# Value bias of an attention kernel: added by VectorE, or by a one-row matmul on TensorE with copies on ScalarE

## The reference, cut to what matters

```python
x = x + jnp.tanh(g_xattn[l]) * xattn_l(_layernorm(x), ctx, ...)
x = x + jnp.tanh(g_ffn[l]) * ffn_l(_layernorm(x), ...)
```

```python
v = (V @ Wv.T + bv).reshape(B, S, H, Dh).transpose(0, 2, 1, 3)
out = softmax(q @ k.T * scale + mask) @ v
```

## Time and profile before

| what | us |
|---|---|
| median of three runs | 1249.05 |
| lowest and highest of the three | 1245.17, 1252.75 |
| the profiled execution | 1246.67 |
| its span, first to last instruction | 1244.9 |

### The profile page before, as it was taken

One profiled execution on the slowest core, in us unless ns is written; L12 is line 12 of the kernel. 1 busy time (PEld: TensorE's weight loads), 2 busy tenths in 40 slices (PEclk: granted clock), 3 DMA queues, 4 the chain that ended last, 5 costly groups with the idle time before them and its releaser, 6 DMA issues. The chain is left out here.

```text
span 1244.9 us, 28580 instructions
## 1 busy us (share of the span) xinstructions
PE 975.1 (78%) x9932; PEld 495.1 (40%) x9932; DVE 847.0 (68%) x1711; ACT 657.4 (53%) x1301; POOL 474.3 (38%) x623
## 2 busy tenths in 40 slices
PE   3788676898389999999778886290788678876997
PEld 2444454455234434444332335170444432333342
DVE  5788637886668667676678966163788669943453
ACT  2277312585255555555427961170288327964886
POOL 4126101563245555555512731405004103312886
PEclk9899868799689999999987995595889978996999
DMA  7662004210044444444254100311531051102332
GB/s 217 218 214 83 1 1 136 62 48 2 1 121 131 129 134 121 133 125 131 74 178 147 37 2 5 91 53 45 183 94 37 2 172 37 36 2 43 102 95 69
DMA packets 111900, 109.31 MB, mean 88 GB/s; under 512 B 16251, under 2 KB 87107, under 8 KB 110883
## 3 DMA queue, kind: packets, MB, share of 16 engines
q1 hardware_dynamic: 109476, 104.57, 28.1%
q0 software_dynamic: 1024, 2.10, 0.6%
q10 hardware_dynamic: 1280, 1.05, 0.4%
HBM read 83.83 MB, written 23.53 MB: 86 GB/s over the span
## 5 line engine op out<-in xcount | busy, mean ns | idle before, releaser
L839 ACT ACTIVATE work<-ps 128x384 f32<-128x384 f32 (+1 forms) x640 | 301.4, 533 | 126.1 <-PE ps L680 79.8
L943 DVE TENSOR_REDUCE bmax<-ps 128x6 f32<-128x768 f32 (+1 forms) x320 | 332.9, 1055 | 35.7 <-PE ps L658 22.9
L1758 POOL TENSOR_TENSOR work<-Ks,work 128x512 f16<-128x512 f32 x196 | 226.8, 1157 | 165.0 <-ACT work L1846 159.8
L1771 PE MATMUL ps<-ao,wf 128*128 128x512 f16 x984 | 247.9, 384 | 7.8 <-DVEq L1870 4.3
L1894 DVE TENSOR_TENSOR Ks<-ps,Qs 128x512 f32<-128x512 f32 x192 | 132.7, 691 | 53.6 <-ACT ps L1838 42.4
L705 PE MATMUL ps<-work,V 128*18 128x256 f32 (+1 forms) x2560 | 161.1, 364 | 0.9 <-ACT work L839 0.9
L1787 PE MATMUL ps<-work,wf 128*128 128x512 f16 x588 | 159.3, 380 | 2.5 <-POOL work L1758 2.5
L669 PE MATMUL ps<-Qs,Ks 32*128 32x256 f16 x640 | 136.1, 289 | 15.6 <-DVE bmax L943 10.2
L1771 PEld LDWEIGHTS ps<-ao,wf 128*128 (+1 forms) x984 | 88.8, 99 | 140.3 <-issue 44.3
L1838 ACT ACTIVATE work<-ps 128x512 f32<-128x512 f32 x132 | 78.8, 597 | 114.8 <-PE ps L1771 112.8
L984 POOL TENSOR_SCALAR mx<-bmax 128x16 f16<-128x16 f32 x80 | 20.3, 254 | 298.2 <-DVE bmax L949 174.0
(11 more groups left out here) (260 smaller groups left out, 1481.3 us busy)
## 6 DMA issues: line engine op xcount, KB each, us to landing
Qs<-scrC SPq DMA_DIRECT2D x256, 128.0 KB, 3.0
Qs<-scrQ SPq DMA_DIRECT2D x40, 256.0 KB, 3.1
Ks<-scrK SPq DMA_DIRECT2D x40, 256.0 KB, 3.3
Qs<-scrC SPq DMA_DIRECT2D x32, 256.0 KB, 3.2
scrK<-work SPq DMA_DIRECT2D x60, 128.0 KB, 2.1
scrQ<-work SPq DMA_DIRECT2D x60, 128.0 KB, 2.6
Qs<-mxT SPq DMA_DIRECT2D x320, 1.0 KB
wf<-in_L_w SPq DMA_DIRECT2D x4, 896.0 KB, 4.7
```

The source lines that it names most:

```text
L839: act.activation(prob[:, g % PROBS, 0:W1], ps[:, ring_bank("score", g), 0:W1], ACT.Exp, scale=float(att["dk"]) ** -0.5).then_inc(exped, 1)
L943: dve.tensor_reduce(bmax[:, n // 4 % 2, 2 * (n % 4):2 * (n % 4) + 2, 0:NB], ps[:, b0:b0 + 2, 0:W1].rearrange("p i (n w) -> p i n w", n=NB) ...
L1758: pool.tensor_tensor(hparts[:, (m + r) % 4, 1, :], weighted(m + r), hparts[:, (m + r) % 4, 0, :], ALU.subtract).then_inc(second, 1)
L1771: ins = pe.matmul(out, weight_parts(which, wpart, j), xh[:, xpart, c * CH:(c + 1) * CH], start=(i == 0), stop=(i == 2))
```

## The change

In each attention stage the bias of the values is no longer added on the way out of PSUM. TensorE starts each chunk's bank with one f32 matmul: a row of 128 ones (`one_row`, a new tile that GpSimd fills in setup) as the weights and the bias row, repeated four times, as 512 columns. It writes bias into the bank for all 128 partitions. The four projections of the chunk then accumulate onto it. What was an addition on VectorE becomes a copy on ScalarE, one per chunk, in ScalarE's list behind its last projection part and ahead of its first exponential.

```diff
+        one_row = sb("one_row", [1, P])
...
+            pool.memset(st["one_row"][:], 1.0)
...
             def project_values(c):
                 wait_low(pe, PARTS.index(("q", c)))
+                bias = rows[0:1, R_OFF["v", a]:R_OFF["v", a] + D].rearrange("p (o d) -> p o d", o=1)
+                pe.matmul(ps[:, 4 + c, :].rearrange("p (t d) -> p t d", t=4), st["one_row"][:], bc(bias, [1, 4, D]),
+                          start=True, stop=False)
                 for k in range(4):
                     t = 4 * c + k
                     ins = pe.matmul(ps[:, 4 + c, k * P:(k + 1) * P], src[:, t * P:(t + 1) * P], w("v"),
-                                    start=True, stop=True)
+                                    start=False, stop=(k == 3))
                 ins.then_inc(v_projected, 1)
...
+            for c in range(NC):
+                act.wait_ge(v_projected, c + 1)
+                act.copy(V[:, 4 * c:4 * c + 4, :, 0:DH],
+                         ps[:, 4 + c, :].rearrange("p (t h d) -> p t h d", t=4, h=H)).then_inc(v_copied, 1)
             for k in range(4):
                 act.wait_ge(written[k], 96)
...
-            def add_value_bias(c):
-                dve.wait_ge(v_projected, c + 1)
-                dve.tensor_tensor(
-                    V[:, 4 * c:4 * c + 4, :, 0:DH],
-                    ps[:, 4 + c, :].rearrange("p (t h d) -> p t h d", t=4, h=H),
-                    bc(rows[:, R_OFF["v", a]:R_OFF["v", a] + D].rearrange("p (o h d) -> p o h d", o=1, h=H),
-                       [P, 4, H, DH]), ALU.add).then_inc(v_copied, 1)
...
-                if 1 <= n <= NC:
-                    add_value_bias(n - 1)
```

## The result

The changed kernel takes 1264.97 us, the median of four runs (1263.26 to 1274.39), against 1249.95 for the kernel before in runs beside it: a ratio of 1.0155, 95% interval 1.0125 to 1.0184. A ratio in this document is the estimate on record, from the executions not slowed by more than 1.5%, and differs a little from the quotient of the two medians, here 1.0120. The forecast was 1254.0 with a range of 1246 to 1262. The measured time lies above the range.

The account below looks back on a forecast made before the run. Stage heads were taken as bound by TensorE up to step 3, then VectorE's reductions. The added matmul, less VectorE's removed additions, delays first scores by 4.95 us in all; +5 on the median gives 1254.0 us, range 1246 to 1262.

Parts of the forecast that it names:

- The bounds of the head: Attention stage heads: TensorE and VectorE nearly even up to step 3, VectorE alone the pace from step 4.
- the sum: First scores later by 0.1, 1.5, 0.9, 2.15 and 0.25 us in the five stages: +4.95 us, 1251.6 for the profiled execution.
- The price of the matmul: One added f32 matmul in each of steps 0 to 3: 0.86 us at full clock, causal step 2.385 us.
- rival (c): The added matmul's weight load is exposed, 1.0 us per matmul: +7.75 us, 1256.8; chance 15%.
- The copies on ScalarE: Four copies per stage from PSUM, 0.585 us each, ahead of the first exponential: cost zero.
- The step that failed: TensorE's clock in the heads: lost in steps 5 to 10, before the scores, a little later than now; nothing gained.
- rival (d): Clock falls inside steps 0 to 3, each step left costs 2.4 us more: +14 us, 1268; chance 10%.
- read as busy share: Reading of the skill's clock rule: the clock stays up once TensorE's idle gap before the filler is gone.
- Rival (a): Clock stays up through the start of the scores, as no idle wait is left: +1 us, 1250; chance 15%.
- Rival (b): Added matmul in steps 0 to 3 nearly hidden, first scores earlier: half of 7.0, -3.5 us, 1245.6; chance 8%.
- the setup matmul of 629 ns: A one-row bf16 matmul of 512 columns in setup, said to run at the low clock; a neighbour for the price.

Follow-up runs that it names:

- full-height kernel: The changed kernel with the added matmul 128 rows high, weights 1/128: 1259.53 us (ratio 1.0134), measured again 1252.16 us (ratio 1.0012).
- wait experiment: The kernel before, with TensorE waiting for a short ScalarE copy ahead of each chunk's projections, no added matmul: 1279.70 us, ratio 1.0286.
- 32 rows: The changed kernel with the added matmul 32 rows high, weights 1/32: 1254.09 us, ratio 1.0050.

## Why the prediction was wrong

**The bounds of the head** were read rightly in the main. Where the clock holds, the sum comes out, in part because errors offset each other. My first scores were to come 16.14 us after step 0 in causal stages and 16.77 in the others; the stages of the changed kernel that did not fall have 15.65 and 16.33 in the first trace. The prediction says that the fifth stage looks the same as the fourth. In the trace of before it does not quite: TensorE waits 0.73 us for VectorE's reductions ahead of the rows of step 2 (1016.31), the wait that comes back at full height. The full-height kernel gives +4.6 and +5.5 us over the five heads, my sum was +4.95, with the fifth stage 1.3 and 0.5 us above the sum and the others up to 0.4 below it. The two measurements of its time differ, 1.0012 and 1.0134 with intervals that do not meet; 1.004 was forecast. Of the 6.0 us between the two profiled executions 4.5 stand in the first 20 score steps, where the low clock lasted 52 us in one and 40 in the other. Why one set of executions should have more of that than the other is open.

**The price of the matmul** was about right in the mean: 0.86 us taken, and the four steps of the first stage now take 9.2 us (43.26 to 52.46), 2.30 a step or 0.775 more than 1.525. With one row that is two errors that nearly cancel. Alone the matmul takes 1.00 us (43.60 to the first projection at 44.60 in step 0, a step of 2.43), which is the price of rival (c). But in steps 1 and 3 it starts 0.03 us after the first row matmul and runs beside the rows, and that step takes 2.17. Step 1 of the first stage:

```profile
45.69 0.23 PE L656 MATMUL ps<-Ks,Qs 32*128 32x128 f16 x2
45.72 0.69 PE L625 MATMUL ps<-rows,one_row 1*128 1x512 f32 x1
```

With full height every step of the first stage is the same, 2.38 us (41.84, 44.22 and 46.60), and 2.385 was forecast. The matmul starts 0.43 us after the rows:

```profile
44.22 0.23 PE L656 MATMUL ps<-Ks,Qs 32*128 32x128 f16 x2
44.65 1.12 PE L625 MATMUL ps<-rows,one_row 128*128 128x512 f32 x2
```

**The copies on ScalarE** cost no time that the traces show, as forecast, but for the short wait of the filler.

**The step that failed is the clock**, and within it rival (d). The sum took all of steps 0 to 3 at full clock, 0.86 us for each added matmul, and put a fall inside them at nothing. Rival (d), by which the one-row matmul "counts as little for the clock", gave the mechanism the right place (inside steps 0 to 3), the right condition and nearly the right price (two low steps in three stages, +14 us on the forecast; the three heads that fell took 5.0 to 5.4 us more than those that did not, 15.7 together). I gave it 10% and left it outside the range. A low step cost 2.0 us more than a full one (4.3 against 2.3), where rival (d) had 2.4, and somewhat more than two steps a stage were low. The reason I gave against it was that steps 0 to 3 ran at full clock with row pieces a third of each step, and that nothing looked close to falling. That was no evidence for the new steps: the trace of before held no step with the added hole in it. What I did have was the kernel's own reaction to idle waits of 1.8 us in every stage, each followed by a fall, and 4 us of fully busy 32-row work at a clock that stayed low. The waits of the other stages are 1.82 to 1.94 us. I used both for the question whether the clock would hold behind step 3, and not for the four times 0.86 us of nearly empty array that the change itself adds. The wait experiment shows that a nearly empty array and an idle one end alike: five falls in five stages with the wait, four in five and six in ten with one row. The profiled execution took 1264.43 us where its sum had 1251.6, 12.8 more, and the 15.7 us of the falls cover that difference.

On the Trainium skill (TensorE: Matmul & The Clock Gate, section "What's actually happening"): read as busy share, its rule would have given no fall at all, since TensorE's busy time was 9.06 of 9.10 us or more in every stretch of the changed kernel that fell. The measurement decides against that reading for one row. For 32 rows the one stretch that fell (9.10 of 9.10 us) goes against it too.

**Rival (a)**, the clock held into the scores, did not happen with the old filler. **Rival (b)** was tried by leaving the matmul out: the heads shrink by 2.7 us of the 7.0 that the formula had, the DMA takes the rest, and the time does not fall. **Rival (c)**, an exposed weight load, is seen behind the one-row matmul. The weight loads of the projections (PEld, line 629) start only at 44.60, with the first projection itself; with full height the first of them starts at 42.80, in the middle of the added matmul and 0.43 us ahead of the projection:

```profile
44.60 0.97 PEld L629 LDWEIGHTS ps<-wp,ctxT 128*128 128x128 f32 x8 [0.76 <-issue]
...
42.80 0.19 PEld L629 LDWEIGHTS ps<-wp,ctxT 128*128 128x128 f32 x1 [0.24 <-issue]
```

The steps in which the one-row matmul runs beside the rows hide this in the mean, so it was not what moved the time.

One row of the prediction is an inference: the setup matmul of 629 ns is called work at the low clock. The record of the granted clock begins at 29 us, after it; the duration fits (512 columns of the filler take 0.63 us at 0.50). Nothing in the sum hangs on it.

## What to carry to other kernels

A thin matmul is charged twice: it occupies TensorE for its columns whatever its height, and to the clock it is close to an idle engine (granted clock 0.66 to 0.71 in stretches where it fell early). Before adding one, look in the profile for how the granted clock reacts to idle waits of the same total length in that stage, and price every following matmul at half rate; if the operation must go to TensorE, spread it over all rows (weights 1/128, replicated operand), which cost 0.3 us more per head in steps 0 to 3 here and kept the clock in ten stages of ten. It was still no faster than the kernel without the change. And before relieving an engine, find what comes last behind it: here a DMA took over at once.

## What the runs showed that I had not expected

- One row against 128 rows, same instruction and columns: 1265.85 us against 1252.16 measured beside each other, six falls in ten stages against none.
- A TensorE that stands still 0.89 us per step in the mean loses its clock inside steps 0 to 3 in five stages of five, the earliest 1.7 us after step 0 (third stage of the wait kernel, with idle time in the projection head before it).
- A one-row matmul can run beside row matmuls that are 32 rows high (starts 0.03 us apart), which the full-height one does not: steps 0 to 3 take 0.3 us more with full height, by the start of reduction 4 (10.09 us after step 0 in place of 9.77).
- Behind a one-row matmul the next weight load starts only with the next matmul, behind a full-height one 0.43 us ahead of it.
- Raising the height of a filler matmul made a kernel slower by 1.1% (0.7 to 1.6) where the clock fell anyway.
